# A Perceiver layer on one core: cross attention of four heads together, with the value strips given to the heads and the keys in a ring of blocks

## The reference

```python
x: (4, 256, 256); ctx: (4, 4096, 192); 16 heads of 16
# 1 cross attention (this is what the change is about)
q = (layernorm(x) @ Wq + bq); k = ctx @ Wk + bk; v = ctx @ Wv + bv      # each head: 16 columns
attn = softmax(clip(einsum('bhqd,bhkd->bhqk', q, k) * scale, -1e4, 1e4))
x = x + einsum('bhqk,bhkd->bqhd', attn, v).reshape(B, 256, 256) @ Wo + bo
# 2 causal self attention over the 256 rows of each batch, q and k normalised per head
# 3 a slot layer: routing (top 8 of 64), a gated update of 64 slots, attention among the slots, outputs
```

## Time and profile before

| | us |
|---|---|
| median of 3 runs | 1366.13 (1365.43 to 1367.64) |
| the profiled execution | 1365.34 |
| its span | 1363.3 |
| PE, DVE, ACT, POOL busy | 1281.0, 929.7, 764.6, 175.4 |

### The profile page before, as it was taken

One profiled execution on the slowest core, in us unless ns is written; L12 is line 12 of the kernel. 1 busy time (PEld: TensorE's weight loads), 2 busy tenths in 40 slices (PEclk: granted clock), 3 DMA queues, 4 the chain that ended last, 5 costly groups with the idle time before them and its releaser, 6 DMA issues.

```text
span 1363.3 us, 33125 instructions
## 1 busy us (share of the span) xinstructions
PE 1281.0 (94%) x10494; PEld 763.2 (56%) x10494; DVE 929.7 (68%) x2033; ACT 764.6 (56%) x1427; POOL 175.4 (13%) x226
## 2 busy tenths in 40 slices
PE   6998999999999999999999999999999887896987
PEld 4674656656666666666566665444444464455534
DVE  6646777777777777777777777888888358534222
ACT  1224666666766766766766776777777712241111
POOL 3503111111111111111111110000000130000000
PEclk8998999999999999999999999999999989997666
DMA  7744546444454444454444443346332000000000
GB/s 193 215 74 105 113 91 122 103 97 107 105 113 101 102 96 107 104 110 105 101 96 108 106 98 63 59 92 156 66 62 39 1 0 1 1 2 0 1 0 31
DMA packets 106004, 110.64 MB, mean 81 GB/s; under 512 B 16822, under 2 KB 98171, under 8 KB 99709
## 3 DMA queue, kind: packets, MB, share of 16 engines
q1 hardware_dynamic: 105862, 109.17, 36.4%
HBM read 81.25 MB, written 27.79 MB: 80 GB/s over the span
## 4 chain that ended last, share of the span: by engine, by line
PE 82%; DVE 9%; ACT 3%; issue 3%; SPq 1%; DMA 1%; POOL 0%; ACTq 0%; DVEq 0%; POOLq 0%
PE acc L1238 18%; PE st L1265 16%; PE mx L1155 16%; PE kps L1146 7%; PE kps L1137 6%; DVE mxp L818 2%; ACT prob L701 2%; PE misc L1248 2%; DVE amax L974 1%; PE st L1146 1%; PE st L1127 1%; PE setB L1424 1%; PE setB L1418 1%; PE misc L1172 1%; PE acc L1137 1%
## 5 line engine op out<-in xcount | busy, mean ns | idle before, releaser
L818 DVE TENSOR_REDUCE mxp<-mx 128x1 f32<-128x512 f32 x1024 | 671.8, 685 | 231.1 <-PE mx L1155 230.5
L626 ACT ACTIVATE prob<-st 128x512 f32<-128x512 f32 x1024 | 585.0, 598 | 293.5 <-PE st L1265 281.7
L1155 PE MATMUL mx<-kst,qst 96*128 96x512 bf16 x1024 | 391.0, 382 | 13.5 <-DMA qst<-qscr 3.6
L1265 PE MATMUL st<-qst,kst 99*128 99x256 bf16 x2048 | 392.6, 274 | 1.4 <-ACT prob L626 1.4
L1265 PEld LDWEIGHTS st<-qst,kst 99*128 99x128 bf16 x2048 | 178.4, 100 | 202.4 <-issue 97.6
L1238 PE MATMUL acc<-prob,vh 128*32 128x256 f32 x4096 | 275.2, 386 | 0.4 <-ACT prob L626 0.4
L1238 PEld LDWEIGHTS acc<-prob,vh 128*32 128x32 f32 x4096 | 106.9, 109 | 121.6 <-issue 68.5
L1155 PEld LDWEIGHTS mx<-kst,qst 96*128 96x128 bf16 x1024 | 98.7, 96 | 54.9 <-DVE mxp L818 34.3
L1146 PE MATMUL kps<-wv,ctx 128*128 128x256 f32 (+1 forms) x376 | 101.6, 392 | 0.0
L489 POOL COPY vh<-v_sb 128x512 f32 (+1 forms) x64 | 39.1, 610 | 482.7 <-PE acc L1238 482.7
L1137 PE MATMUL kps<-ctx,wk 128*128 128x256 f32 (+1 forms) x368 | 95.7, 381 | 3.7 <-DMA ctx<-in_ctxT 3.7
(11 more groups left out here) (362 smaller groups left out, 1070.7 us busy)
## 6 DMA issues: line engine op xcount, KB each, us to landing
kst<-kscr SPq DMA_DIRECT2D x64, 384.0 KB, 4.6
kst<-kscr SPq DMA_DIRECT2D x192, 128.0 KB, 5.1
kscr<-kparts SPq DMA_DIRECT2D x108, 192.0 KB, 2.5
ctx<-in_ctxT SPq DMA_DIRECT2D x93, 128.0 KB, 2.0
ctx<-in_ctxT SPq DMA_DIRECT2D x93, 64.0 KB, 2.2
kscr<-o_sb SPq DMA_DIRECT2D x20, 192.0 KB, 2.5
qst<-qscr SPq DMA_DIRECT2D x192, 8.0 KB, 4.1
v_sb<-in_ctxT SPq DMA_DIRECT2D x16, 128.0 KB, 2.4
```

What stands on the lines that cost most here:

```text
L626: act.activation(prob[:, s % 8, :], st[bank_of[s]][:, :], ACT.Exp).then_inc(exp_done, 1)
L818: dve.reduce_max(mxp[:, par, s // 8, s % 8:s % 8 + 1], mxb[s % 2][:, :], AX.X).then_inc(max_red, 1)
L1155: pe.matmul(mxb[s % 2][:, :], qst[0:96, slot, qt * P:(qt + 1) * P], kst[0:96, slot, n * 512:(n + 1) * 512], start=True, stop=True).then_in ...
L1265: mm = pe.matmul(st[bank_of[s]][:, n * T:(n + 1) * T], kst[0:99, u, (2 * s + n) * P:(2 * s + n + 1) * P], qst[0:99, u, :], start=True, sto ...
```

## The change

- Four heads of one batch (a quad) are worked together, 64 units each (UQ): unit t is two key tiles of head t % 4. The strips of acc are now the heads: strip j holds 17 columns, 16 values and the sum. Values lie in v4 as (tile, head, 17), the ones set once, so POOL's copy and vh are gone; finish only turns the accumulator.
- Keys come as blocks of 512 keys for four heads, rows of 1 KB, into a ring of 12 blocks; queries in 12 slots, per quad.
- Value products of 8 units (16 products) follow at t % 8 == 2. Half projections follow t % 8 in (4, 7), keys in even blocks and values in odd ones.
- Maxima run 76 units ahead (AHEAD). The steps for the shift, the flag, the low row and the division are made once per quad, the shift and the low row in pairs of heads.
- Exponentials have 16 buffers, eight of them in xn and xnT.
- The program is unrolled. Small tensors of the later layers share space with others; their constants are set by POOL in quad 12.
- The beginning: x and the query weights are loaded from ACT's queue, batch 0 first; its queries are made behind three chunks and split at once; the first block is loaded after two chunks; key chunks 7 to 15, the other queries, the value chunks and key chunks 16 to 19 are made between the maxima. The second bf16 part of the keys is made by POOL instead of DVE.

```diff
-NH = B * H
 C2 = C - P
 CH = 256
 NCH = B * S // CH
 KLEAD, VLEAD = 20, 17
-ST = 16
-LEAD = 4
+NQ = B * H // 4
+UQ = 64
+NU = NQ * UQ
+LD = 12
+AHEAD = UQ + LD
+RB = 12
+NX = 16
...
-        kst = sb("kst", [P, 4, S], BF16)
-        qst = sb("qst", [P, 4, T], BF16)
+        v_raw = sb("v_raw", [P, 64 * H * VW])
+        v4 = v_raw[:, :].rearrange("p (t h d) -> p t h d", t=64, d=VW)
+        kst = sb("kst", [P, 4, RB * 512], BF16)
+        qst = sb("qst", [P, 12, T], BF16)
         prob = sb("prob", [P, 8, 512])
-        vh = sb("vh", [P, 2, 32, 32])
+        xn_p = xn[:, :, :].rearrange("p t d -> p (t d)").rearrange("p (n q) -> p n q", q=512)
+        xnT_p = xnT[:, :, :].rearrange("p c t -> p (c t)").rearrange("p (n q) -> p n q", q=512)
+
+        def exps(u):
+            n = u % NX
+            return prob[:, n, :] if n < 8 else xn_p[:, n - 8, :] if n < 12 else xnT_p[:, n - 12, :]
...
+            def load_block(n):
+
+                q, k = n // 8, n % 8
+                b, r0 = q // 4, 64 * (q % 4)
+                for c in (16 * b + 2 * k, 16 * b + 2 * k + 1):
+                    sp.wait_ge(*written(c))
+                src = kscr[r0:r0 + 64, :, b * S + k * 512:b * S + (k + 1) * 512]
+                cols = slice(n % RB * 512, n % RB * 512 + 512)
+                done = block_in(n)[0]
+                if 4 <= n < RB:
+                    sp.wait_ge(done, 64 * (n // 4))
+                sp.dma_start(kst[0:48, :, cols], src.rearrange("(j d) r t -> (d r) j t", j=4)).then_inc(done, 16)
+                for m, r in enumerate((0, 1, 0)):
+                    sp.dma_start(kst[48 + 16 * m:64 + 16 * m, :, cols],
+                                 src[:, r:r + 1, :].rearrange("(j d) r t -> (d r) j t", j=4)).then_inc(done, 16)
...
+            write_k(0)
+            write_k(1)
+            sp.wait_ge(ctx_in[1], 32)
+            load_early(12, 16, 1)
+            write_k(2)
+            write_k(3)
+            load_block(0)
+            write_q(0)
+            write_k(4)
+            write_k(5)
+            load_q(0)
+            load_block(1)
+            write_k(6)
+            sp.dma_start(wv[:, 0, :], a["L0_xattn_Wv"][0:P, :]).then_inc(w_in, 16)
+            sp.dma_start(wv[0:C2, 1, :], a["L0_xattn_Wv"][P:C, :]).then_inc(w_in, 16)
+            sp.dma_start(wv[C2:C2 + 1, 1, :], a["L0_xattn_bv"].rearrange("(o n) -> o n", o=1)).then_inc(w_in, 16)
+            write_k(7)
+            load_block(2)
+            for n in range(4, 8):
+                write_k(2 * n)
+                write_k(2 * n + 1)
+                load_block(n - 1)
...
+            for q in range(NQ):
+                for k in range(8):
+                    sp.wait_ge(st_ps, UQ * q + 8 * k + 8)
+                    if 8 * q + k + RB < 8 * NQ:
+                        load_block(8 * q + k + RB)
+                    if k == 0 and 3 <= q + 2 < NQ:
+                        load_q(q + 2)
...
+            def k_split(c):
+
+                pool.wait_ge(k_r, c + 1)
+                pool.tensor_copy(parts_of(c)[:, :, 1, :], kres[:, c % 2, :, :]).then_inc(k_2, 1)
+                pool.wait_ge(k_2, c + 1)
+                pool.tensor_tensor(parts_of(c)[:, :, 2, :], kres[:, c % 2, :, :], parts_of(c)[:, :, 1, :],
                                    ALU.subtract).then_inc(k_3, 1)
...
-            for c in range(KLEAD):
-                pool.wait_ge(k_2, c + 1)
-                pool.tensor_tensor(early_parts(c)[:, :, 2, :], kres[:, c % 2, :, :], early_parts(c)[:, :, 1, :],
-                                   ALU.subtract).then_inc(k_3, 1)
-            pool.wait_ge(v_out, VLEAD)
-            pool.wait_ge(rest_set, 16)
-            copy_vh(0, 0, 0, 0)
...
+            for n in range(NU):
+                q, t = n // UQ, n % UQ
+                act.wait_ge(st_ps, n + 1)
+                if n >= NX and n % 8 == 0:
+                    act.wait_ge(pv_done, n // 8 - 1)
+                act.activation(exps(n), st[n % 3][:, :], ACT.Exp).then_inc(exp_done, 1)
+                if t == 2:
+                    low_bound(q, 0)
+                if t == 4 and q > 0:
+                    save_acc(q - 1)
+                if t == 6:
+                    low_bound(q, 1)
+                if n >= 8 and t % 8 == 0:
+                    c = k_job((n - 8) // UQ, (n - 8) % UQ // 8)
+                    if c is not None:
+                        k_first(c)
+                    c = v_job((n - 8) // UQ, (n - 8) % UQ // 8)
+                    if c is not None:
+                        v_copy(kps, c)
+                if t == 60 and q + 1 < NQ:
+                    shift_rows(q + 1, 0)
+                if t == 62 and q + 1 < NQ:
+                    shift_rows(q + 1, 1)
...
+            for m in range(AHEAD):
+                reduce_unit(m)
+                if m % 2 == 1 and 3 <= m < 21:
+                    k_rest(7 + (m - 3) // 2)
+                if m in (18, 24):
+                    turned_early(m // 3 - 5)
+                if m % 2 == 1 and 61 <= m < 69:
+                    k_rest(16 + (m - 61) // 2)
+                shift_step(0, m - LD)
...
+            def max_unit(n):
+
+                q, m = n // UQ, n % UQ
+                if m == 0:
+                    pe.wait_ge(qst_in, 112 * (q + 1))
+                if n % 8 == 0:
+                    pe.wait_ge(*block_in(n // 8))
+                wait(pe, max_red, n - 1)
+                j, qt, at = m % 8 // 2, m % 2, n // 8 % RB * 512
+                pe.matmul(mxb[n % 2][:, :], qst[0:96, 4 * (q % 3) + j, qt * P:(qt + 1) * P],
+                          kst[0:96, j, at:at + 512], start=True, stop=True).then_inc(max_ps, 1)
...
+            def score_unit(n):
+
+                q, t = n // UQ, n % UQ
+                s, j = t // 4, t % 4
+                wait(pe, exp_done, n - 2)
+                if t in (0, 2):
+                    pe.wait_ge(shift_set, 2 * q + t // 2 + 1)
+                for h in range(2):
+                    at = (8 * q + s // 2) % RB * 512 + (2 * s + h) % 4 * P
+                    mm = pe.matmul(st[n % 3][:, h * T:(h + 1) * T], kst[0:99, j, at:at + P],
+                                   qst[0:99, 4 * (q % 3) + j, :], start=True, stop=True)
+                mm.then_inc(st_ps, 1)
...
+            def turn_shift(q, pair):
+
+                if pair == 0:
+                    pe.wait_ge(m_3, q + 1)
+                    wait(pe, head_out, 2 * (q - 1))
+                    wait(pe, low_set, 2 * q)
+                else:
+                    pe.wait_ge(shift_set, 2 * q + 1)
+                for jj in range(2):
                     for qt in range(QT):
+                        mm = pe.matmul(misc[:, (2 * jj + qt) * P:(2 * jj + qt + 1) * P], spad[:, 2 * pair + jj, qt, :],
+                                       identb[:, :], start=True, stop=True)
+                mm.then_inc(shift_ps, 1)
...
+            def spread_low(q, pair):
+
+                if pair == 0:
+                    pe.wait_ge(flag_abs, q + 1)
+                    pe.wait_ge(shift_set, 2 * q + 2)
+                else:
+                    pe.wait_ge(low_set, 2 * q + 1)
+                at = 4 * (q % 3) + 2 * pair
+                pe.matmul(misc[:, :], shrow[0:99, :], qst[0:99, at:at + 2, :].rearrange("p j t -> p (j t)"),
+                          start=True, stop=True).then_inc(low_ps, 1)
+
+            def values(q, k):
+
+                pe.wait_ge(exp_done, UQ * q + 8 * k + 8)
+                pe.wait_ge(clip_done, UQ * q + 8 * k + 8)
+                if q % 4 == 0:
+                    pe.wait_ge(v_out, 16 * (q // 4) + 2 * k + 2)
+                    pe.wait_ge(vcol_set, 1 if q < 4 else 2)
+                if k == 0:
+                    wait(pe, acc_out, q)
+                for n in range(4 * k, 4 * k + 4):
+                    for j in range(4):
+                        h = 4 * (q % 4) + j
+                        mm = pe.matmul(acc[32 * j:32 * j + VW, 0:T], v4[:, q // 4 % 2 * 32 + n, h, :],
+                                       exps(4 * (n // 2) + j)[:, n % 2 * T:(n % 2 + 1) * T],
+                                       start=(n == 0), stop=(n == 31), skip_group_check=True)
+                mm.then_inc(pv_done, 1)
+
+            def finish(q):
+
+                pe.wait_ge(acc_out, q + 1)
+                wait(pe, head_out, 2 * q)
+                pe.wait_ge(low_set, min(2 * q + 4, 2 * NQ))
+                for qt in range(QT):
+                    mm = pe.matmul(misc[:, qt * P:(qt + 1) * P], accs[:, qt * P:(qt + 1) * P], ident[:, :],
+                                   start=True, stop=True)
+                mm.then_inc(fin_ps, 1)
...
             pe.wait_ge(rows_set, 4)
...
+            pe.wait_ge(w_in, 16 * 3)
+            for c in range(3):
                 for g in range(2):
                     early_k(c, g)
...
+            pe.wait_ge(consts, 3)
+            turn_early(0)
+            pe.wait_ge(consts, 5)
             for g in range(2):
...
+                early_k(3, g)
+            queries(0)
+            for c in range(4, 7):
```

(117 more changed lines are left out.)

1026 lines of the change are left out of this document (437 added, 589 removed).

## The result

| | before | after |
|---|---|---|
| median | 1366.13 (1361.29 to 1368.17, 5 runs) | 1372.96 (1372.46 to 1374.62, 5 runs) |
| ratio | | 1.0061, 95% interval 1.0041 to 1.0081 |
| span of the profiled execution | 1363.3 | 1370.6 |

The changed kernel is slower by 0.6%.

The account below looks back on a forecast made before the run. PE was taken as the bound, with DVE's reductions setting a second rhythm. The terms +17.6 - 4 + 6 - 1 - 3 - 8 + 1.4 made +9 on 1366.1, so 1375 us; forecast range 1366 to 1388, given as 1354 to 1394.

Parts of the forecast that it names:

- to the first score: Beginning: first score at 128 us (bounds 120 and 138) instead of 110.4, +17.6.
- first quad (head 0's stall gone): Start of the scores: the 3.7 us wait for late context data goes, the table load stays: -4 (bounds -6 and 0).
- quads 1 to 10: Main loop: a quad takes 63.6 us, before 63.1; +6 us over eleven quads.
- quad 11: The quad that still projects values, at the end of the main loop: -1 us.
- quad 12 until maxima end: Quads without projections: 6.6 us per block against 6.80, -3 us over the 180 units to where maxima end.
- last 76 units: End, units without maxima: 52.5 us against 60.5 before, -8 (bounds -12 and -5).
- behind the last score: End: the last value burst waits for all 8 units, +1.4 us.
- The run of three: Block of 8 units: the third maximum waits for DVE, 0.28 us, twice per block; 7.78 against 7.44 before.
- The small steps: Closing turn, low rows and shift turns, once per quad: 1.4 us (bounds 0.8 and 3), before 3.56.
- the residue behind a reduction that waits: Beginning: a key chunk waits for the residue DVE makes after a maximum; 2.66 us per two units.
- the rival about them: Key blocks: 1 KB rows land after their 12 units, or the first query block comes late: 1395 and over; chance 0.13.
- The rival of the strips: Value bursts: strips of 17 don't run side by side, 6.9 us instead of 1.72, +650, total 2020; chance 0.02.

Follow-up runs that it names:

- e1: Changed kernel, but DVE's reduction of a maximum reads 256 of the 512 columns: 1308.16 us, ratio 0.9584 to the kernel before.
- e4: Changed kernel with value products every 4 units and runs of two maxima in quads 0 to 11 and 15: 1344.50 us, ratio 0.9846 to the kernel before.
- e9: As e8, but value products every 8 units in quads 0 to 14, some half projections split into quarters, all runs of two: 1318.05 us, ratio 0.9661.
- e7: Kernel before, with three of a head's four half projections one step later, making runs of three maxima: 1405.88 us, ratio 1.0312.
- e3: Changed kernel, but in the beginning DVE makes a chunk's key residue one reduction earlier: 1366.79 us, ratio 1.0014 to the kernel before.
- e6: Kernel before, with key chunk 20's context load issued ahead of the writes of chunks 16 to 19 on SP's queue: 1359.32 us, ratio 0.9946.
- e2: Changed kernel, with the 13 late weight loads issued two behind each key block instead of in one go: 1366.49 us, ratio 1.0014 to the kernel before.
- e8: Changed kernel with e2, e3 and e4 together and value products one group later: 1325.00 us, ratio 0.9692 to the kernel before.

## Why the prediction was right

1375 was forecast and 1372.96 measured. By its own terms (starts of the scores of both profiled executions; the last column is the growth of the gap between them):

| term | forecast | measured |
|---|---|---|
| to the first score | +17.6 | +16.8 |
| first quad (head 0's stall gone) | -4, +0.5 | -7.7 |
| quads 1 to 10 | +0.5 each, +5 | -0.14 each after the first, -1.8 |
| quad 11 | -1 | -0.8 |
| quad 12 until maxima end | -3 | +6.4 |
| last 76 units | -8 | -6.7 |
| behind the last score | +1.4 | +0.9 |
| sum | +9 | +7.3 |

- **The run of three was right and its price too.** 7.79 per block against 7.78; e1 takes the stall away by its cause, e4 and e9 by the order, e7 brings it into the kernel before. By 176 x 0.28 = 49 us it is the largest single cost of the new order; runs of two, which pay for a second burst instead, give 28 back.
- **The small steps were mis-sized.** 1.4 per quad was forecast. In the changed kernel 62.93 less 8 x 7.79 leaves 0.6, since most of them stand in stalls; without stalls they are 1.3 (e4) and 1.9 (e9). That turned +0.5 per quad into -0.14.
- **The beginning was right in its parts.** First maximum 36.3 against 38, two units with a chunk 2.79 against 2.66, maxima with a value half 1.09 each. The mechanism named (the residue behind a reduction that waits) is shown by e3.
- **Head 0 was mis-sized.** I took the table load as staying and the wait as its bare 3.7. e6 shows 7.0 for the wait and the slow clock behind it. The share was misread too: 129.61 is not the end of head 0 but twelve of its 16 steps. Its next head starts at 134.23, so head 0 is 8.0 over its 15.77, not some 5.
- **The transfers did decide in one place,** which the rival about them did not name: 13 weight loads in quad 12, between key blocks that the ring wants every 6.6 us. Before, a head's keys were asked for 20 steps ahead of its first maximum, and now a block 12 units ahead. e2 prices it at 5.4 us. Without it, +1.0 stands against my -3. There the sum was also careless: 22.5 blocks x -0.2 and 1.2 of small steps in 2.8 quads make about -1.
- **The end was right but for the clock.** In the last 76 units of this execution stands a stretch at half clock, which e2 and e3 with the same order don't have there; their last units take 50.9 instead of 52.4, which would have made the term -8.2:

```profile
1050.90:1054.30 3.40, 3.23 (x20) 1.92 (x24) 0.56 (x3) 2.09 (x5) 0.00 (x0) 0.50 0.00 0
```
- The errors had both signs (-4.2 and -6.8 against +9.4 and +1.3), so that the total is within 3 us of the forecast is luck in part: its parts don't deserve it.
- The rival of the strips: strips of 17 columns at partitions 0, 32, 64 and 96 ran side by side, 1.85 for the burst of 16 products, where 32-wide ones took 1.00 for 8. The burst's row above refutes it.

## What to carry to other kernels

With two banks between a fast producer and a slower consumer, what counts is the length of the runs between pauses, not the busy shares: here the third maximum of a run cost 0.28 us, 176 times, with the consumer busy 70% of that stage. Before merging or moving the work that makes the pauses, write out one block's starts. And when a deep buffer is replaced by a shallow ring, look for whatever else uses the same queue once.

## What the runs showed of the hardware

The same instructions at the end of the kernel took 81.2 us in one execution and 74.6 in another (changed kernel and e8, from the same product to the end):

```profile
1289.40:1370.60 81.20, 68.14 (x195) 34.16 (x194) 16.86 (x42) 8.40 (x14) 0.00 (x0) 0.63 0.04 13
```
```profile
1250.10:1324.70 74.60, 61.34 (x195) 31.71 (x194) 16.86 (x42) 8.41 (x14) 0.00 (x0) 0.71 0.04 14
```

The granted clock is 0.63 in the one and 0.71 in the other. PE's busy time differs by 6.8 and its idle time by 0.2, so the difference is the clock's. Behind the last score as a whole it is 282.2 against 274.3. So a part of up to 8 us of a single profiled span is not the kernel's. In quads 1 to 10 of both kernels the clock is 1.00; the terms of the first score, of the first quad, of quad 12 and of the last 76 units hold stretches at half clock.

A short pause was enough for such a stretch: behind PE's wait of 1.81 us in e4 the clock was 0.50 for 3.4 us, behind 3.81 in the changed kernel it was at or near half for 5.5 (e2 takes both away and gives 5.4 back), and behind 3.66 in the kernel before for 7.2. The waits cost 1.4 to 1.9 times their length.

In the unrolled kernels POOL took 2.5 to 3.4 us from its branch to the semaphore that it raises behind it, and 4.8 to 5.4 in quad 8, in each of the eight executions kept of them. In the kernel before, with hardware loops, it took some 0.5. Why quad 8 differs stays open. PE had to wait for it only when the burst came close (e4).
